# Three attention layers of a fused kernel: the softmax sums' and outputs' transfers on ScalarE's queue, and the output bias on GpSimd

## The reference, cut to what matters

```python
q = layernorm(x) @ Wq + bq            # 16 heads of width 16
k, v = ctx @ Wk + bk, ctx @ Wv + bv   # 1601 keys; the second layer turns q and k (rotary embedding)
e = exp(scale * q @ k.T - max)        # softmax over the keys
out = (e @ v) / sum(e)
x = x + tanh(g) * (out @ Wo + bo)
```

## Time and profile before

| | before |
|---|---|
| runs, median (lowest to highest) | 3891.18 us (3888.99 to 3891.73) |
| profiled execution, its own time | 3877.86 us |
| its span, first to last instruction | 3876.7 us |
| TensorE clock granted, mean | 0.938 |
| PE busy | 3409.0 us (88%) |
| VectorE (DVE) busy | 2180.8 us (56%) |
| ScalarE (ACT) busy | 2033.8 us (52%) |
| GpSimd (POOL) busy | 653.1 us (17%) |
| chain that ended last | PE 65%, DVE 14%, DMA 7%, issue 5%, POOL 4%, ACT 3%, SPq 2% |

### The profile page before, as it was taken

The page is one execution under the profiler, slowest core; times in us unless marked ns, Lnnn a source line. Parts: engine busy times, 40 slices in busy tenths (PEclk is TensorE's granted clock), DMA queues, the critical chain, the costliest instruction groups (busy, mean ns, idle before and its releaser), DMA issues.

```text
span 3876.7 us, 52367 instructions
## 1 busy us (share of the span) xinstructions
PE 3409.0 (88%) x18396; PEld 1775.9 (46%) x18396; DVE 2180.8 (56%) x3567; ACT 2033.8 (52%) x4490; POOL 653.1 (17%) x700
## 2 busy tenths in 40 slices
PE   5899999978588899997799699889986979987997
PEld 3333333325332233332588333223325956677996
DVE  6767676736757677873401477768843033265334
ACT  2566666653236566766333167567771322244664
POOL 2111111001125331000302131210002020022331
PEclk8999999999779999999899699999997989998998
DMA  8132323105664343310865555654207521042555
GB/s 191 43 102 63 102 63 102 24 26 185 165 181 118 94 106 74 61 24 14 276 219 176 170 157 119 173 115 100 78 10 277 177 89 56 13 139 88 179 179 177
DMA packets 314686, 456.02 MB, mean 118 GB/s; under 512 B 66315, under 2 KB 234195, under 8 KB 312251
## 3 DMA queue, kind: packets, MB, share of 16 engines
q1 hardware_dynamic: 243382, 292.39, 27.5%
q0 software_dynamic: 29568, 104.65, 7.9%
q10 hardware_dynamic: 41477, 55.63, 5.1%
HBM read 292.46 MB, written 153.91 MB: 115 GB/s over the span
## 4 chain that ended last, share of the span: by engine, by line
PE 65%; DVE 14%; DMA 7%; issue 5%; POOL 4%; ACT 3%; SPq 2%; ACTq 0%; POOLq 0%; DVEq 0%
PE pv L1334 14%; PE m L1298 10%; DVE mxp L1181 10%; PE s L1320 9%; PE h L2794 5%; PE y L2802 5%; PE h L2368 4%; PE y L2377 3%; PE y L1779 2%; PE s L1759 2%; PE s L1265 2%; PE m L1342 1%; ACT e_t L1412 1%; PE s L1282 1%; DMA ot<-sums 1%
## 5 line engine op out<-in xcount | busy, mean ns | idle before, releaser
L1181 DVE TENSOR_REDUCE mxp<-m 128x1 f32<-128x802 f32 x1536 | 1447.7, 985 | 522.4 <-PE m L1298 519.8
L1412 ACT ACTIVATE e_t<-s 128x512 f32<-128x512 f32 (+1 forms) x2496 | 1338.9, 600 | 569.3 <-PE s L1320 568.6
L1298 PE MATMUL m<-kaug,qaug 97*128 97x401 bf16 x3072 | 811.4, 347 | 111.1 <-DVE mxp L1181 60.9
L1320 PE MATMUL s<-qaug,kaug 100*128 100x512 bf16 (+1 forms) x2496 | 857.4, 386 | 22.7 <-ACT e_t L1412 18.4
L1334 PE MATMUL pv<-e_t,v 128*32 128x512 f32 (+1 forms) x4992 | 670.2, 609 | 0.2
L1320 PEld LDWEIGHTS s<-qaug,kaug 100*128 100x128 bf16 (+1 forms) x2496 | 228.1, 99 | 715.6 <-ACT e_t L1412 496.6
L1298 PEld LDWEIGHTS m<-kaug,qaug 97*128 97x128 bf16 x3072 | 273.8, 100 | 521.3 <-DVE mxp L1181 280.5
L127 POOL TENSOR_TENSOR rstd<-rstd,mhalf 128x16 f32<-128x16 f32 (+2 forms) x9 | 24.2, 2687 | 1203.2 <-DVE rstd L120 1203.2
L2864 ACT ACTIVATE ez<-h,b 128x128 f32<-128x128 f32 x440 | 119.8, 387 | 160.0 <-PE h L2794 160.0
L1334 PEld LDWEIGHTS pv<-e_t,v 128*32 128x32 f32 (+1 forms) x4992 | 98.6, 108 | 214.6 <-ACT e_t L1412 155.5
L2255 DVE SCALAR_TENSOR_TENSOR y<-y,b 128x256 f32<-128x256 f32 x39 | 16.6, 424 | 309.5 <-PE y L2377 309.5
(11 more groups left out here) (370 smaller groups left out, 3560.6 us busy)
## 6 DMA issues: line engine op xcount, KB each, us to landing
w<-in_L_w POOLq DMA_DIRECT2D x78, 1024.0 KB, 5.2
w<-in_L_w SPq DMA_DIRECT2D x24, 1024.0 KB, 12.8
xregion<-zero ACTq DMA_DIRECT2D x10, 2056.0 KB, 12.5
kaug<-kparts SPq DMA_DIRECT2D x16, 1200.8 KB
kaug<-kready SPq DMA_DIRECT2D x32, 600.4 KB
kaug<-kready SPq DMA_DIRECT2D x16, 1200.8 KB
vn<-values SPq DMA_DIRECT2D x8, 1536.0 KB
values<-p_vb ACTq DMA_DIRECT2D x21, 512.0 KB, 4.5
```

The costliest lines, as they stand in the source:

```text
L1181: dve.tensor_reduce(a.mxp[:, u.g % 2, half, n:n + 1], a.m_slot[u.m % 2][:].rearrange("p (a n) -> p a n", a=2)[:, :, 0:PIECE + 1], AX.XY, A ...
L1298: m = pe.matmul(slot[:, 512 * k:512 * k + PIECE + 1], a.qaug[0:R_MAX, u.g, j, P * qc:P * qc + P], a.kaug[0:R_MAX, u.g, j, k0:k0 + PIECE + ...
L1320: pe.matmul(slot[0:KW[u.k], :], a.kaug[0:R_ALL, u.g, u.j, P * u.k:P * u.k + KW[u.k]], a.qaug[0:R_ALL, u.g, u.j, :], start=True, stop=True) ...
L1412: act.activation(a.e_t[0:KW[u.k], e % 2, u.j, :], a.s_slot[u.s % 3][0:KW[u.k], :], ACT.Exp).then_inc(s_free.sem, 1)
```

## The change

- `head_sum_sp` and `head_spread_sp` are gone from SyncE. Their five moves, the store and the load are issued by ScalarE, in three units: "sum", a new "low" (the store) and "spread" (the load). ScalarE now waits in its own order for the reciprocal (before the store) and for the store's landing (before the load).
- The sums' three transfers count on a semaphore of their own, `summed`; "rec" waits for the first of them alone. "norm" waits for both semaphores, and so does the copy to `z`.
- `NORM_STEPS` goes from 5 to 6, which moves the places: by the same rule of spreading they are n = 8 (sum), 15 (rec), 22 (low), 30 (spread), 44 (norm); with outputs 8, 12, 16, 20 and 28, and the outputs from 32 on.
- GpSimd adds `bob` to x, once in a layer and before the outputs: four instructions of 128 x 1024. VectorE's wait and add behind each output go, 48 in all, and so does the last one's `x_done`; the fence waits for `m_free` instead.
- Some semaphores are merged or renamed (`b_scaled` and `bv_made` to `b_made`, `ident` to `tables`).

```diff
-NORM_STEPS = 5
-MOVES = 1 + HG + 2
+NORM_STEPS = 6
...
-        for kind in ("sum", "rec", "spread"):
+        for kind in ("sum", "rec", "low", "spread"):
             self.add(kind, b=b, g=g)
             yield
...
-        ends = ["x_done", "s_free", "z_full", "r_full", "td", "moved"]
+        ends = ["m_free", "s_free", "z_full", "r_full", "td", "moved", "summed"]
...
 def head_pool(kn, a):
...
+        elif u.kind == "bias":
+
+            pool.wait_ge(b_made.sem, b_made.at(3))
+            for b in range(B):
+                xb = kn.x[:, TT * b:TT * b + TT, :]
+                pool.tensor_tensor(xb, xb, a.bob[:].rearrange("p (t n) -> p t n", t=1).to_broadcast([P, TT, D]),
+                                   ALU.add).then_inc(biased.sem, 1)
...
 def head_dve(kn, a):
...
-            kn.settle(dve, "dve_own", dve.tensor_scalar(a.bob[:], a.bob[:], a.gate, None, ALU.mult))
+            dve.tensor_scalar(a.bob[:], a.bob[:], a.gate, None, ALU.mult).then_inc(b_made.sem, 1)
...
         elif u.kind == "rec":
-            dve.wait_ge(moved.sem, moved.at(MOVES * u.n + 1 + HG))
+            dve.wait_ge(summed.sem, summed.at(3 * u.n + 1))
             dve.reciprocal(a.rc[:], a.rc[:]).then_inc(r_full.sem, 1)
         elif u.kind == "norm":
-            dve.wait_ge(moved.sem, moved.at(MOVES * 2 * (u.n + 1)))
+            dve.wait_ge(moved.sem, moved.at(HG * 2 * (u.n + 1)))
+            dve.wait_ge(summed.sem, summed.at(3 * 2 * (u.n + 1)))
...
         elif u.kind == "out":
             xt = x[:, u.b * TT + u.k, :]
+            if u.k == 0:
+                dve.wait_ge(biased.sem, biased.at(u.b + 1))
             dve.wait_ge(m_full.sem, m_full.at(u.m + 1))
             dve.scalar_tensor_tensor(xt, a.m_slot[u.m % 2][:, 0:D], a.gate, xt, ALU.mult, ALU.add).then_inc(m_free.sem, 1)
-            dve.wait_ge(m_free.sem, m_free.at(u.m + 1))
-            i = dve.tensor_tensor(xt, xt, a.bob[:], ALU.add)
-    i.then_inc(x_done.sem, 1)
...
 def head_act(kn, a):
...
             if n:
-                act.wait_ge(moved.sem, moved.at(MOVES * (n - 1) + 1 + HG))
+                act.wait_ge(moved.sem, moved.at(HG * n))
+                act.wait_ge(summed.sem, summed.at(3 * (n - 1) + 1))
             act.copy(a.z[:], a.pv[:]).then_inc(z_full.sem, 1)
+
+def head_sum_act(kn, a, u):
+    act, z_full, m_full = kn.nc.scalar, kn.sema("z_full"), kn.sema("m_full")
+    moved, summed = kn.sema("moved", DMA), kn.sema("summed", DMA)
+    act.wait_ge(z_full.sem, z_full.at(u.n + 1))
+    if u.n:
+        act.wait_ge(moved.sem, moved.at(HG * u.n))
+        act.wait_ge(summed.sem, summed.at(3 * u.n))
...
+    act.dma_start(a.rc[:], a.z[HD::P // HG, :]).then_inc(summed.sem, DMA)
+    for j in range(HG):
+        to, of = HG * HD * (u.g % 2) + HD * j, P // HG * j
+        act.dma_start(a.op[to:to + HD, u.g // 2, :], a.z[of:of + HD, :]).then_inc(moved.sem, DMA)
+
+def head_low_act(kn, a, u):
+    act, r_full, summed = kn.nc.scalar, kn.sema("r_full"), kn.sema("summed", DMA)
+    sums = kn.dram["sums"]
+    act.wait_ge(r_full.sem, r_full.at(u.n + 1))
+    act.dma_start(sums.rearrange("j (a c) -> (j a) c", a=P // HG), a.rc[:]).then_inc(summed.sem, DMA)
+
+def head_spread_act(kn, a, u):
+    act, summed = kn.nc.scalar, kn.sema("summed", DMA)
+    act.wait_ge(summed.sem, summed.at(3 * u.n + 2))
+    lo = HG * HD * (u.g % 2)
+    act.dma_start(a.rs[lo:lo + HG * HD, u.g // 2, :],
+                 kn.dram["sums"].rearrange("j (a n) -> j a n", a=1).to_broadcast([HG, HD, T])).then_inc(summed.sem, DMA)
```

More of the change, by code:

```diff
@@ L497, in add @@
             u.m = self.next("m")
-        if kind in ("pv", "turn", "sum", "rec", "spread", "norm", "take", "peak"):
+        if kind in ("pv", "turn", "sum", "rec", "low", "spread", "norm", "take", "peak"):
             u.n = self.next(kind)
@@ L778, in head_attention @@
             sig(name, DMA).close(n)
-        sig("moved", DMA).close(MOVES * NG * B)
-        ends = ["x_done", "s_free", "z_full", "r_full", "td", "moved"]
+        sig("moved", DMA).close(HG * NG * B)
+        sig("summed", DMA).close(3 * NG * B)
+        ends = ["m_free", "s_free", "z_full", "r_full", "td", "moved", "summed"]
         if not ready:
@@ L889, in head_sp @@
                 a.arrived[u.b, u.g + n, "k" if "k" in u.what else "q"] = (u.by, a.dmas[u.by])
[L890 to L893, removed]
         elif u.kind == "turn":
@@ L898, in head_sp @@
                              a.tm[16 * k:16 * k + 16, :]).then_inc(td.sem, DMA)
[L901 to L931, removed]
 def head_ready_sp(kn, a, n_of):
@@ L1055, in head_ready_sp @@
             values_of(u.b + 1)
[L1056 to L1059, removed]
         elif u.kind == "turn":
@@ L1139, in head_dve @@
     turns = units("turn")
-    ot_full, moved = kn.sema("ot_full"), kn.sema("moved", DMA)
+    ot_full, moved, summed, biased = kn.sema("ot_full"), kn.sema("moved", DMA), kn.sema("summed", DMA), kn.sema("biased")
     ld_q = kn.sema("ld_q", DMA)
@@ L1236, in head_pe @@
     if not a.ready:
-        ident = kn.sema("ident", DMA)
+        ident = kn.sema("tables", DMA)
         pe.wait_ge(ident.sem, ident.at(1))
@@ L1348, in head_act @@
     s_full, s_free, m_free, pv_done = (kn.sema(n) for n in ("s_full", "s_free", "m_free", "pv_done"))
-    z_full, v_taken, b_scaled, filled = (kn.sema(n) for n in ("z_full", "v_taken", "b_scaled", "filled"))
+    z_full, v_taken, b_made, filled = (kn.sema(n) for n in ("z_full", "v_taken", "b_made", "filled"))
     ld_k = kn.sema("ld_k", DMA)
     rope = a.rope is not None
-    moved = kn.sema("moved", DMA)
+    moved, summed = kn.sema("moved", DMA), kn.sema("summed", DMA)
     if not a.ready:
@@ L1413, in head_act @@
                            ACT.Exp).then_inc(s_free.sem, 1)
+        elif u.kind == "sum":
+            head_sum_act(kn, a, u)
+        elif u.kind == "low":
+            head_low_act(kn, a, u)
+        elif u.kind == "spread":
+            head_spread_act(kn, a, u)
         elif u.kind == "pv" and u.k == KT - 1:
@@ L1417, in head_act @@
             if n:
-                act.wait_ge(moved.sem, moved.at(MOVES * (n - 1) + 1 + HG))
+                act.wait_ge(moved.sem, moved.at(HG * n))
+                act.wait_ge(summed.sem, summed.at(3 * (n - 1) + 1))
             act.copy(a.z[:], a.pv[:]).then_inc(z_full.sem, 1)
+def head_sum_act(kn, a, u):
+    act, z_full, m_full = kn.nc.scalar, kn.sema("z_full"), kn.sema("m_full")
+    moved, summed = kn.sema("moved", DMA), kn.sema("summed", DMA)
+    act.wait_ge(z_full.sem, z_full.at(u.n + 1))
+    if u.n:
+        act.wait_ge(moved.sem, moved.at(HG * u.n))
+        act.wait_ge(summed.sem, summed.at(3 * u.n))
+    if u.b:
+        outs = [x for x in a.plan.units if x.kind == "out" and x.b == u.b - 1]
+        act.wait_ge(m_full.sem, m_full.at(outs[-1].m + 1))
+    elif a.p and u.g == 0:
+        for f in range(a.p.RING):
+            kept = kn.sema(f"p_k{f}", DMA)
+            act.wait_ge(kept.sem, kept.at(a.p.stores[f]))
+    act.dma_start(a.rc[:], a.z[HD::P // HG, :]).then_inc(summed.sem, DMA)
[13 more added lines that the diff above has]
+                 kn.dram["sums"].rearrange("j (a n) -> j a n", a=1).to_broadcast([HG, HD, T])).then_inc(summed.sem, DMA)
 def clear_act(kn, a, nth):
@@ L2897, in first_loads_act @@
     act, w = kn.nc.scalar, a.w
-    ident, mask, gates = kn.sema("ident", DMA), kn.sema("mask", DMA), kn.sema("gates", DMA)
+    ident, mask, gates = kn.sema("tables", DMA), kn.sema("mask", DMA), kn.sema("gates", DMA)
     ld_q, rows, filled = kn.sema("ld_q", DMA), kn.sema("rows", DMA), kn.sema("filled")
@@ L2922, in setup_dve @@
     dve, cst = kn.nc.vector, kn.cst
-    ident, ready = kn.sema("ident", DMA), kn.sema("set")
+    ident, ready = kn.sema("tables", DMA), kn.sema("set")
     dve.memset(cst["ones"][:], 1.0)
@@ L2967, in setup_close @@
         kn.sema(name).close(1)
-    for name, n in (("const", 6), ("gates", 2), ("ident", 1), ("x_loaded0", 1), ("x_loaded1", 1), ("mask", 1), ("maskrow", 1)):
+    for name, n in (("const", 6), ("gates", 2), ("tables", 1), ("x_loaded0", 1), ("x_loaded1", 1), ("mask", 1), ("maskrow", 1)):
         kn.sema(name, DMA).close(n)
```

21 lines of the change are left out of this document (10 added, 11 removed).

## The result

The changed kernel takes 3981.76 us (median of 4 runs, 3976.97 to 3984.66) against 3891.45 before: a ratio of 1.023, interval 1.0214 to 1.0246. It is slower by 90 us, where I had forecast 42, and 2 us outside my range.

A forecast was written before the change was run, and what follows sets the result against it. PE was taken to bound plain stretches, ScalarE's spare time counting only while PE misses no slot. Terms +63.6, +20, -28.2, -4, -3.6, -6.2 gave +41.6 us: 3919.5 profiled, 3933 at the median, range 3860 to 3980.

The forecast's parts named there:

- row of five: Five moves issued on ScalarE's queue delay the exponentials and PE: +63.6 us over 45 sums, bounds 0 and 138.
- clearings ahead of the store: Third layer: the store lands behind the clearing on ScalarE's queue and ScalarE waits: 8 x 2.5 = +20 us.
- waits at "norm": VectorE's waits ahead of norm in three long stretches shrink or go: -28.2 us together, bounds 16.5 and 39.
- bias -3.6: Stretches with outputs: bias on GpSimd saves 0.4 us in each of 9, 3.6 us.
- "rec" -4: Stretch of 46.50 us: the reciprocal waits for one move, not five, a gain of 4 us, bounds 0 and 7.5.
- layers' ends: End of each layer: store 1.6 us earlier and last bias add of 0.42 us gone, 3 x 2.05 = 6.2 us less.
- That is 1.5 us of PE standing still: Plain stretch: exponential 9 comes late behind the five moves, score matmul 12 waits, and PE cannot win back 1.5 us.
- the third rival, the clock: PE's wait also delays VectorE's maxima and the clock falls: near 3 us per sum, 3995 us in all; chance 0.14.
- the argument that waits there were 2.5 us and more: Point against the clock falling: the VectorE waits after which it had fallen were 2.5 us and more.
- I leave 6 and 5 us of wait: Two third-layer stretches: the load stands behind a clearing, so waits at norm remain; only 7.4 and 4.3 us go.
- the rule cited in the prediction: Transfers of all engines share 16 DMA engines, so another issuing engine saves issue time only; the reciprocal's 4 us stay lost.
- At most 0.8 can go; 9 stretches x 0.4: Stretches with outputs have 4.9 us more, PE 4.1 of them; moving the bias to GpSimd saves 3.6 us.

The follow-up runs named there:

- e2: Changed kernel with the five moves still on ScalarE's queue, one behind each of exponentials 8 to 12: 3877.88 us, ratio 0.9976 to the kernel before.
- e10: Changed kernel with two moves issued behind exponential 8, two behind 9, one behind 10: 3877.51 us, ratio 1.0003 to the kernel before.
- e7: Changed kernel with three moves issued behind exponential 8 and two behind 9: 3931.8 us, ratio 1.0118 to the kernel before.
- e3: Changed kernel with each third-layer clearing issued behind the load of the sums, five moves still in a row: 3932.26 us, ratio 1.012 to the kernel before.
- e5: Changed kernel with the five moves back on SyncE's queue and each clearing behind the load: 3839.93 us, ratio 0.9874 to the kernel before.
- e11: Kernel before with only the sums' own semaphore, so the reciprocal waits for one landing instead of five: 3868.36 us, ratio 0.9973.
- e8: Kernel before with only the changed places (NORM_STEPS 6, an empty step behind rec), transfers on SyncE, bias on VectorE: 3899.97 us, ratio 1.0021.
- e4: Kernel before with only the bias moved to GpSimd, added once in a layer: 3882.3 us, ratio 0.9987.
- e6: Changed kernel with one move behind each of exponentials 8 to 12 on ScalarE and the clearings behind the load: 3844.88 us, ratio 0.988 to the kernel before.

## Why the forecast had the sign and not the size

The forecast's terms, and what the profiles show for each. The row of five is the 45 stretches of the changed kernel less those of e2; the next four are e2 less before. The forecast's 3.6 for the bias was for all nine stretches with outputs. The right column adds up to the 106.8 us between the two spans, of which some 16 come from which executions were profiled: the medians are 90 us apart.

| term | forecast | measured |
|---|---|---|
| row of five, 45 stretches | +63.6 | +101.3 |
| clearings ahead of the store, 8 stretches | +20 | +31.0 |
| waits at "norm", 3 stretches | -28.2 | -23.8 |
| stretches with outputs, 6 others: bias -3.6, places 0 | -3.6 | -7.2 |
| all other stretches: "rec" -4 | -4 | +7.1 |
| outside of the stretches: layers' ends | -6.2 | -1.6 |
| sum | +41.6 | +106.8 |

**The row of five.** The mechanism was the one forecast. Plain stretches 40.67 where I said 40.5, 1.63 us of idle PE where I said 1.5, five issues of 3.09 us in the row shown. The step that failed is "That is 1.5 us of PE standing still" taken as the whole price of a row: the 32 at 1.5, and the prices of the others taken from it. It had no term for what the clock does behind the pause. Of the 45, twelve cost 1.7 us at full clock. Six others with the same row and work cost 3.2 to 5.2, all at a granted clock under 1. The eight with a clearing cost 20.2 us together instead of 12. The three stretches beside the projection of keys cost 4.4 to 5.5 us each instead of 1.5 (exponentials there wait until 172.98 for a row begun at 169.06, which took 3.87 us), but the three behind them 0.4 us together. The last stretches cost 3.1 instead of 2.2, and those of g = 0 with projected queries 5.6 us together instead of 0.

So the third rival, the clock, was no alternative to my case but came on top of it. In the changed kernel 46 pauses of PE of 0.9 us or more ahead of a score matmul end with an exponential; before there was none. I read the granted clock over the 4.5 us behind each. Behind the three of 1.07 to 1.14 us it stayed full. Of the 27 pauses of 1.58 to 1.80 us six were followed by part of the time at 1.2 GHz. Of the 16 from 1.89 to 2.98 us fourteen were. The price of a drop is the difference of the two plain stretches above, 42.15 - 40.67 = 1.5 us; twenty of them are 30 us, an estimate for rows and clearings together. I had the rows for that, in the clock of the long stretches of the earlier trace rows, and used them only for waits of VectorE; the argument that waits there were 2.5 us and more did not hold, since pauses of 1.6 us were enough in six cases. Why they were in these six and not in the other 21 is not shown.

**The clearings.** The arithmetic of the wait held: the load is issued 3.3 to 3.6 us behind the last exponential in the eight stretches (forecast 3.4), and TensorE's pause is 2.6 to 3.0 us (forecast 2.5). What failed is again that this pause was taken for the whole price. Two of the eight show the difference:

```profile
2522.85:2566.41 43.56, 38.41 (x222) 11.88 (x221) 31.25 (x40) 28.73 (x54) 9.97 (x12) 1.00 0.69 151
2416.43:2462.60 46.17, 41.31 (x222) 12.18 (x221) 31.34 (x40) 28.73 (x54) 0.00 (x0) 0.93 0.41 88
```

Both have the row and pauses of 2.7 us at the load. The first keeps the full clock and takes 2.9 us more than the plain 40.67. The second, with a drop behind the row and one behind the load, takes 5.5 more. Without the row such a stretch costs 3.9 us more than before (e2, mean of 8), with both 6.4, where I had 4.0. That is also where much of the ratios of the cut rows comes from: from e10 to e7 the plain stretch grows by 0.5 us, but the eight with a clearing from 41.4 to 44.6 in the mean; seven of the eight pass at full clock in e10, one in e7.

**The waits at "norm".** In the second layer the term held: 69.19 became 51.23 (52.7 forecast), and the wait of 13.80 us is one of 0.20. In the third layer the step "I leave 6 and 5 us of wait" failed. VectorE still waited 9.71 and 10.52:

```profile
2496.05 0.69 DVE L1173 TENSOR_TENSOR ot<-ot 128x512 f32<-128x512 f32 x1 [9.71 <-DMA ot<-sums]
...
2691.52 0.69 DVE L1173 TENSOR_TENSOR ot<-ot 128x512 f32<-128x512 f32 x1 [10.52 <-DMA ot<-sums]
```

With the clearing behind the load the first of these waits is gone and the second 2.4 us (e3) and 3.2 us (e5); the stretches fall to 46.9 and 50.1, and to 45.3 and 49.4. So the wait after is not the wait of before: then, the load stood behind the store of split queries on SyncE's queue; now it stands behind 2 MB of zeros on ScalarE's. I saw the second, and priced it too low.

**"rec".** e11 shows what waiting for one landing gives, 3.2 of the forecast 4 us. The changed kernel doesn't keep it: the same stretch takes 45.99 us against 46.50, and VectorE waits 3.35 us for the one landing. ScalarE issues that move at 1219.15, beside SyncE's fetch of keys (timelines of SyncE's queue, ScalarE's queue and VectorE):

```profile
1218.46 0.43 SPq L934 DMA_DIRECT2D kf<-keys  x1
1218.93 1.43 SPq L936 DMA_DIRECT2D kr<-keys  x2
...
1219.15 0.60 ACTq L1410 DMA_DIRECT2D rc<-z  x1
...
1231.02 0.25 DVE L1169 RECIPROCAL rc<-rc 128x16 f32<-128x16 f32 x1 [3.35 <-DMA rc<-z]
```

The reciprocal starts 11.9 us behind the move. In e11, where SyncE issues the move ahead of the fetches, it is 9.3 us. So another queue did not bring the sums sooner here, which is what the rule cited in the prediction gave for this term.

**Bias and places.** The step "At most 0.8 can go; 9 stretches x 0.4" put a gain on the wrong edit. The adds are worth nothing in the stretches; the later places, for which the sum had no term, are worth 1.2 to 2.1 us each (e8). Which of them does it (norm at 28 instead of 25, outputs from 32 instead of 30) was not tried.

**The layers' ends.** "rec" comes 2.5 us behind the last copy instead of 5.0, as forecast. The outputs come only 0.9 to 1.2 us earlier, since the way from "rec" to "norm" grew from 5.0 to 5.2 us to 6.4 to 6.8. The long sections between the attentions differ by 6 to 7 us between before and e4 or e11, which share no edit there. I can't assign that, and it is of the size of the smaller effects here.

**What stays open.** e5 and e6 end level, with what is late next in different places. In e5 the moves stand behind fetches of queries and keys in SyncE's queue, and VectorE waits 8.65 us for the sums at 1372, in the stretch of 50.57 us above. In e6 that stretch takes 40.79, but one of the second layer's takes 42.2, and two of the third layer's 42.3 and 45.5. A kernel with both gains was not made.

## What to carry to other kernels

An engine that is idle a quarter of the time can still set the pace when it feeds the bound engine through three slots: add up, instruction by instruction, when each slot is wanted and when it is freed. Issues of transfers on such an engine cost nearly nothing one at a time, beside an instruction that runs anyway, and 100 us in all when they stood five in a row. And before small transfers that someone waits for join a queue, look at what that queue carries: here the place of twelve issues of 2 MB, some 4 us ahead of them in eight stretches, was worth 33 to 50 us.

## What the runs showed that I had not expected

- Issuing one of these moves on ScalarE's queue takes 0.5 to 0.6 us, but runs beside the exponential ahead of it: with one issue each, exponentials come every 0.63 us, against 0.5 without.
- Pauses of TensorE of only 1.6 us were followed by the clock of 1.2 GHz in 6 of 27 cases, of 1.9 us and more in 14 of 16. The same work with the same pause takes 40.67 us in one place and 42.15 in another.
- The store of 8 KB was followed by its load 10.0 to 10.3 us later when it was issued 3.5 to 4 us behind 2 MB on its own queue (eight stretches of the changed kernel), and 7.8 to 9.1 us later when issued 1 us behind 2 MB on the other queue (the same eight before, is one). Without a clearing it was 1.4 us before. What decided was where the waiting stood: ahead, it had been SyncE that waited, and then ScalarE, with the exponentials behind it. The Trainium skill ("DMA: Bandwidth & Descriptors", section on issuing engines not being separate DMA queues) says that issuing on several engines saves only the issue time, "usually small relative to the DMA itself". These rows agree that the other queue gives little. But the issue time, some 3.1 us a group, moved onto ScalarE and was the larger part of the result.
